# Graph block on one Trainium2 core: attention weights multiplied together before the items, slice tokens summed in turned form, a rewritten slice attention

## The reference, cut to what matters

```python
fx_mid = (x @ W_fx + b_fx).reshape(B, N, H, D).transpose(0, 2, 1, 3)
x_mid = (x @ W_x + b_x).reshape(B, N, H, D).transpose(0, 2, 1, 3)
slice_weights = jax.nn.softmax((x_mid @ W_slice + b_slice) / temp, axis=-1)
slice_norm = slice_weights.sum(axis=2)
slice_token = jnp.einsum('bhnc,bhng->bhgc', fx_mid, slice_weights)
slice_token = slice_token / (slice_norm[..., None] + 1e-05)
q = slice_token @ W_q
k = slice_token @ W_k
v = slice_token @ W_v
attn = jax.nn.softmax(jnp.einsum('bhgc,bhkc->bhgk', q, k) * SCALE, axis=-1)
out_slice = jnp.einsum('bhgk,bhkc->bhgc', attn, v)
out_x = jnp.einsum('bhgc,bhng->bhnc', out_slice, slice_weights)
return out_x.transpose(0, 2, 1, 3).reshape(B, N, INNER) @ W_out + b_out
```

## Time and profile before

| | us |
|---|---|
| median of 3 runs | 1682.46 (1680.82 to 1684.41) |
| the profiled execution's own time | 1682.33 |
| its span, first to last instruction | 1680.6 |
| PE busy | 1391.1 (83%) |
| VectorE (DVE) busy | 1310.9 (78%) |
| POOL busy | 1111.6 (66%) |
| ScalarE (ACT) busy | 665.2 (40%) |

### The profile page before, as it was taken

How to read it: one execution, slowest core, us unless ns; L and a number is a source line. 1 busy time by engine, 2 the same in 40 slices (tenths; PEclk the granted TensorE clock), 3 DMA queues, 4 the chain that set the end, 5 groups by cost and what they waited for, 6 DMA issues and landing times. The chain is left out here.

```text
span 1680.6 us, 27556 instructions
## 1 busy us (share of the span) xinstructions
PE 1391.1 (83%) x8473; PEld 1102.6 (66%) x8473; DVE 1310.9 (78%) x3978; ACT 665.2 (40%) x1867; POOL 1111.6 (66%) x1196
## 2 busy tenths in 40 slices
PE   5399989984788889888888888888989888886798
PEld 3277767763567777766666666666767666664587
DVE  8999879973588887888888888888787887873244
ACT  0144333420455454555455454455454544531000
POOL 1078888886777777777777777777777777720000
PEclk9699999985799998999999899899998999997599
DMA  9011112113444444444444444444444444512722
GB/s 231 9 58 53 43 41 65 48 37 87 118 124 123 123 125 124 123 123 127 119 123 123 118 122 123 123 122 124 124 121 124 121 121 116 150 51 68 267 74 72
DMA packets 106322, 180.11 MB, mean 107 GB/s; under 512 B 29183, under 2 KB 77694, under 8 KB 106175
## 3 DMA queue, kind: packets, MB, share of 16 engines
q0 software_dynamic: 44384, 113.26, 26.0%
...
...
## 5 line engine op out<-in xcount | busy, mean ns | idle before, releaser
L1043 POOL DMA_INDIRECT big<-node_table,rest x850 | 826.6, 972 | 245.4 <-issue 231.9
L1114 PE MATMUL psum<-big 128*125 128x257 f32 x1700 | 437.2, 415 | 73.7 <-DVE big L1615 73.7
L1114 PEld LDWEIGHTS psum<-big 128*125 128x125 f32 x1700 | 342.9, 207 | 139.6 <-DVE big L1615 80.5
L1262 ACT ACTIVATE rest<-big,rest 128x125 f32<-128x125 bf16 x850 | 268.3, 490 | 165.8 <-DVE rest L1563 164.7
L1615 DVE TENSOR_SCALAR big<-big,rest 128x125 f32<-128x125 bf16 x850 | 172.8, 293 | 0.0
L327 POOL DMA_INDIRECT edge_groups<-rest x112 | 143.9, 1285 | 27.2 <-issue 21.8
L1570 DVE TENSOR_REDUCE rest<-rest 128x125 f32<-128x2125 f32 x50 | 118.3, 2367 | 32.2 <-ACT rest L1262 32.2
L1253 ACT COPY big<-psum 125x1024 bf16<-125x1024 bf16 x150 | 103.8, 763 | 38.4 <-PE psum L1091 38.4
L1149 PE MATMUL psum<-big 125*128 125x256 f32 x416 | 101.1, 387 | 0.0
L1135 PE MATMUL psum<-rest,big 128*125 128x512 f32 x208 | 99.7, 601 | 0.0
L1759 PE MATMUL psum<-rest,big 128*125 128x256 f32 x400 | 88.7, 384 | 2.0 <-DVE rest L1812 2.0
...
## 6 DMA issues: line engine op xcount, KB each, us to landing
big<-node_table,rest POOLq DMA_INDIRECT x850
...
```

The lines of the kernel that those rows point to most:

```text
L1043: pool.indirect_dma_start(Gt[:, u, q * TW:(q + 1) * TW], None, table, bass.IndirectOffsetOnAxis(ap=item[:, u, 2 * q:2 * q + 1], axis=0)).t ...
L1114: mm = pe.matmul(bank[bAgg][0:R, 0:D + 1], P[:, u, q, :], Gt[:, u, q * TW:q * TW + D + 1], start=q == 0, stop=q == Q - 1)
L1262: act.activation(V[:, :, q], O[:, u, q, 0:R], ACT.Copy, scale=score[:, u, q:q + 1]).then_inc(s_v, 1)
```

## The change

Six things differ; line numbers in this section's rows are those of each kernel's own file.

- The seven attention weights are loaded by SP at the start of the items stage, behind the loads for the `W_x` fold and ahead of the items' own loads, and no longer after the last item.
- Ahead of the items TensorE turns `Wq`, `Wk`, `Wv`, makes `Wqk` (the product of query and key weights) and `Wvo` (value weights times output weights, per head), which ScalarE copies over `Wq` and `Wo`. The zeroing of the accumulators waits for that.
- `tokens` holds a 128-column piece of `y` as stationary operand and moves the 512 columns of `L`: two matmuls, and the sum is turned (256 x 512). The four zero matmul records that closed the sum (L1237) are gone.
- The attention needs no turning of the tokens. The norm is spread to rows by matmuls with the identity, `sT` is divided by it in one pass; `Wqk` replaces the queries and keys, `Wvo` the values and the output projection; the division by the softmax total goes to the copy of `M2`. VectorE's steps go from 21 to 14, with ScalarE taking half of some copies.
- All 50 loads of weight tiles are issued by SP, and the output stores by ScalarE.
- `total` and `res` share memory with the attention's tiles.

```diff
-        bfx, spare_row = rows2[0:1], rows2[32:33]
+        bfx, spare_row = rows2[0:FH, 0:G], rows2[32:33]
         Wq, Wk, Wv = a.take(G, G), a.take(G, G), a.take(G, G)
         Wo = a.take(G, FH, D)
+        Wqk, Wvo = Wq, Wo
...
+            turned_w = b.take(G, 3, G)
...
+                    attention_weights = ((Wfx, W_fx.rearrange("(c p) n -> p c n", p=128)), (bfx, b_fx.rearrange("(h c) -> h c", h=FH)), (Wq, W_q),
+                                         (Wk, W_k), (Wv, W_v), (Wo, W_out.rearrange("(h c) d -> c h d", h=FH)),
+                                         (bout, row(b_out).to_broadcast([R, D])))
+                    for to, of in attention_weights:
+                        sp.dma_start(to, of).then_inc(aw_in, 16)
...
+                    pe.wait_ge(aw_in, 112)
+                    for i, w in enumerate((Wq, Wk, Wv)):
+                        mm = pe.transpose(bank[7][0:G, i * G:(i + 1) * G], w, ident[0:G, 0:G])
+                    mm.then_inc(fw_psum, 1)
+                    pe.wait_ge(folded, 1)
+                    pe.matmul(bank[7][0:G, 256:256 + G], turned_w[:, 0, :], turned_w[:, 1, :], start=True, stop=True
+                              ).then_inc(fw_psum, 1)
+                    for i in range(IC):
+                        if i == IC - 1:
+                            pe.wait_ge(folded, 2)
+                        pe.matmul(bank[(0, 1, 2, 7)[i]][0:G, :], turned_w[:, 2, :],
+                                  Wo[:, 2 * i:2 * i + 2, :].rearrange("c h d -> c (h d)"), start=True, stop=True
+                                  ).then_inc(fw_psum, 1)
                     pe.wait_ge(fw_done, 19)
+                    pe.wait_ge(folded, 2 + IC)
...
-                    def tokens(n, u):
-
-                        for c in range(IC):
-                            mm = pe.matmul(bank[bSum + c // 2][:, (c % 2) * D:(c % 2 + 1) * D], L[:, c * 128:(c + 1) * 128],
-                                           y[:, u, :], start=False, stop=False, skip_group_check=True)
+                    def tokens(n, u, last=False):
+
+                        for c in range(DC):
+                            mm = pe.matmul(bank[bSum + c][:, :], y[:, u, c * 128:(c + 1) * 128], L, start=False, stop=last,
+                                           skip_group_check=True)
                         mm.then_inc(sum_psum, 1)
...
-                    tokens(last + 1, (TAIL + 1) % U)
-                    for b in range(2):
-                        mm = pe.matmul(bank[bSum + b][:, :], zero_row[:, 0:128], zero_row, start=False, stop=True,
-                                       skip_group_check=True)
-                    mm.then_inc(sum_psum, 1)
-                    pe.wait_ge(sum_psum, last + 3)
+                    tokens(last + 1, (TAIL + 1) % U, True)
+                    pe.wait_ge(sum_psum, last + 2)
...
+                    act.wait_ge(fw_psum, 3)
+                    act.copy(turned_w.rearrange("c i n -> c (i n)"), bank[7][0:G, 0:3 * G]).then_inc(folded, 1)
+                    act.wait_ge(fw_psum, 4)
+                    act.copy(Wqk, bank[7][0:G, 256:256 + G]).then_inc(folded, 1)
+                    for i in range(IC):
+                        act.wait_ge(fw_psum, 5 + i)
+                        act.copy(Wvo[:, 2 * i:2 * i + 2, :].rearrange("c h d -> c (h d)"), bank[(0, 1, 2, 7)[i]][0:G, :]
+                                 ).then_inc(folded, 1)
...
...
         with ExitStack() as _:
             a = Arena(rest, after_m2, REST_W)
...
+            tail_at = a.at
+            tokT = a.take(128, DC, INNER)
+            sT, sA, P, PT = (a.take(G, INNER) for _ in range(4))
+            Z = a.take(G, FH, D)
+            den_row, norm_rows = a.take(G, INNER), a.take(FH, INNER)
             den = a.take(128, IC)
...
+            ptop, ptot, pinv = a.take(G, FH), a.take(G, FH), a.take(128, IC)
+            ap, ad, ae = sem("attn_psum"), sem("attn_done"), sem("attn_copied")
             OB = 5
+            a = Arena(rest, tail_at, REST_W)
             total, res = a.take(R, OB, D), a.take(R, OB, D)
             o_psum, o_sum, o_done = (sem(n) for n in ("o_psum", "o_sum", "o_done"))
             o_out = [sem(f"o_out{u}") for u in range(OB)]
 
...
             with nc.Block() as block:
                 @block.sync
                 def _(sp):
...
                     for t in range(T):
...
+                        job = sp.value_load(job_of[0:1, t:t + 1], min_val=1, max_val=ITEMS + 1)
+                        sp.dma_start(SW[:, t].rearrange("p c r -> p (c r)"),
+                                     sw_store[bass.ds(job, 1)].rearrange("c p f -> (c p) f")).then_inc(sw_in[t // SW_GROUP], 16)
+
+                def head(h):
                     return slice(h * G, (h + 1) * G)
+
+                half = INNER // 2
 
                 @block.tensor
                 def _(pe):
...
                     for i in range(IC):
...
+                        mm = pe.matmul(bank[1][0:FH, i * 128:(i + 1) * 128], slice_norm[:, i:i + 1].to_broadcast([128, FH]),
+                                       ident, start=True, stop=True)
                     mm.then_inc(ap, 1)
...
+                    pe.wait_ge(ad, 2)
+                    for i in range(IC):
+                        mm = pe.matmul(bank[0][0:G, i * 128:(i + 1) * 128], den[:, i:i + 1].to_broadcast([128, G]), ident,
+                                       start=True, stop=True)
+                    mm.then_inc(ap, 1)
+                    pe.wait_ge(ad, 4)
+                    pe.matmul(bank[2][0:G, :], bfx, norm_rows, start=True, stop=False, skip_group_check=True)
+                    pe.wait_ge(ae, 1)
                     for h in range(FH):
                         for c in range(DC):
...
+                            mm = pe.matmul(bank[2][0:G, head(h)], Wfx[:, c, head(h)], tokT[:, c, head(h)], start=False,
+                                           stop=c == DC - 1, skip_group_check=True)
                     mm.then_inc(ap, 1)
...
+                    pe.wait_ge(ad, 5)
+                    pe.matmul(bank[3][0:G, 0:half], Wqk, sT[:, 0:half], start=True, stop=True)
+                    pe.matmul(bank[4][0:G, 0:half], Wqk, sT[:, half:], start=True, stop=True).then_inc(ap, 1)
+                    pe.wait_ge(ad, 6)
+                    pe.wait_ge(ae, 3)
                     for h in range(FH):
...
+                        mm = pe.matmul(bank[0][0:G, head(h)], sA[:, head(h)], sT[:, head(h)], start=True, stop=True)
                     mm.then_inc(ap, 1)
+
+                    def values(i):
+
+                        for h in (2 * i, 2 * i + 1):
+                            mm = pe.matmul(bank[4 + i][0:G, (h % 2) * D:(h % 2 + 1) * D], sT[:, head(h)], Wvo[:, h, :],
+                                           start=True, stop=True)
+                        mm.then_inc(ap, 1)
+
+                    values(0)
+                    values(1)
+                    pe.wait_ge(ae, 4)
+                    for h in range(FH):
+                        mm = pe.transpose(bank[1][0:G, head(h)], P[:, head(h)], ident[0:G, 0:G])
+                    mm.then_inc(ap, 1)
+                    values(2)
+                    values(3)
                     pe.wait_ge(ad, 10)
                     for h in range(FH):
...
+                        lo, i = (h % 2) * G, h // 2
+                        if h % 2 == 0:
+                            pe.wait_ge(ae, (5 + i if i < 2 else 8))
+                        mm = pe.matmul(bank[2 + i][lo:lo + G, 0:D], PT[:, head(h)], Z[:, h, :], start=True, stop=True)
+                        if h % 2:
+                            mm.then_inc(ap, 1)
+                    pe.wait_ge(ad, 14)
+                    pe.wait_ge(ae, 10)
                     for t in range(T):
                         if t % SW_GROUP == 0:
                             pe.wait_ge(sw_in[t // SW_GROUP], 16 * SW_GROUP)
@@ -1762,9 +1788,25 @@
 
                 @block.scalar
                 def _(act):
...
+                    act.copy(tokT[:, 1, :], bank[bSum + 1][:, :]).then_inc(ae, 1)
+                    act.wait_ge(ap, 2)
+                    act.copy(den_row, bank[0][0:G, :]).then_inc(ae, 1)
+                    act.wait_ge(ap, 4)
+                    act.copy(sA[:, half:], bank[4][0:G, 0:half]).then_inc(ae, 1)
+                    act.wait_ge(ad, 8)
+                    act.activation(P, P, ACT.Exp, scale=SLICE_SCALE).then_inc(ae, 1)
+                    for i in range(IC):
+                        act.wait_ge(ap, (6 + i if i < 2 else 7 + i))
+                        act.copy(Z[:, 2 * i:2 * i + 2, :].rearrange("k h d -> k (h d)"), bank[4 + i][0:G, :]).then_inc(ae, 1)
                     act.wait_ge(ad, 12)
...
+                    for i in range(2, IC):
+                        act.wait_ge(ap, 11 + i)
+                        act.activation(M2[:, i, :], bank[2 + i][:, 0:D], ACT.Copy, scale=pinv[:, i:i + 1]).then_inc(ae, 1)
+                    for t in range(T):
+                        act.wait_ge(o_done, t + 1)
```

(22 more changed lines are left out.)

83 lines of the change are left out of this document (1 added, 82 removed).

## The result

The changed kernel takes 1659.0 us in the median of 5 runs (1656.9 to 1663.1), the kernel before 1683.1 beside it: the ratio is 0.986, 95% interval 0.984 to 0.988. Two repeats of it gave 0.985 (0.983 to 0.987) and 0.986 (0.984 to 0.987). The forecast was 1666.1 with a range from 1660 to 1671. The sign and the place of the gain were right; it is 24 us and not 16.

The account below looks back on a forecast made before the run. POOL's gathers were taken to end the items, with the output's TensorE matmuls last in the chain. Gains of 1.2 + 1.2 + 13.0 + 0.8 = 16.2 off 1682.33 gave 1666.1 us, range 1660 to 1671.

Parts of the forecast that it names:

- What bounds the kernel: Whole kernel: POOL's gathers set when the items end; the output's 88.75 us of TensorE matmuls can only start earlier.
- The attention: Between items and output: with fewer VectorE steps, 40.5 us becomes 27.5 at the low clock, gain 13.0, 1.5 either way.
- The clock at its start: First matmuls of the attention: the last tokens can leave TensorE's clock high for the three spreads, gain 0.8, between 0 and 2.6.
- Rival 1: Attention: TensorE runs warm at 2.4 GHz; wholly, 1653.5 us, chance 0.06; for a part, 1659 to 1663, chance 0.12.
- Closing records: End of the items stage: without the four zero records VectorE sets the end, gain 1.2, between 1 and 1.6.
- Hold-up by the late loads: Last items: attention weight loads delayed gathers near 1445; loading them earlier gains 1.2, between 0 and 3.
- Products: Ahead of the items: weight products make the first item 2.3 us late, POOL's slack covers it, cost 0.
- the other engines alone need 20.4 us an item: Items: period of the engines besides POOL, against POOL's 21.8, so they regain 1.4 us with every item.
- rival 4: Items: turned tokens or a colder clock lift the engines' period past POOL's 21.8 us; from 22.2 no gain; chance 0.02.
- Loads and stores: Around attention and output: one queue feeds the output's loads fast enough, cost 0; ScalarE's store issues cost 0.1.

## Why the prediction was right and where it was wrong

- **What bounds the kernel** held: no matmul of the output got shorter (387 ns in the mean for 384), POOL never waited for a buffer, and the output has no wait for loads (0.6 us of idle time in all).
- **The attention, 13.0**: right in mechanism and nearly in size, 14.4. It was worked out for the low clock, and at the low clock the new sequence takes 26.15 us where I had 27.5; `W_fx` was the piece too dear, 5.0 for a measured 3.7: I had taken 0.62 a head from a sequence in which L1727 follows each head's L1726.
- **The clock at its start, 0.8**: the step that failed. I bounded it by 0 and 2.6, the three spreads alone. It measured 26.15 less 20.2, **5.9 us**: the clock stayed at 1.00 for 9 us, through the spreads, `W_fx`, `Wqk` and the scores. The row that I held against it, 5.00 of 5.00 busy at 0.50, shows only that a low clock can stay low. That it would be high at 1546 the rows could have told: the closing records ran four times 512 columns in 1.98 us, the high pace, right up to the pause of 3 us that the change removes. That it would stay high for 9 us they could not: with the closing records put back it was as high at the start and fell 0.5 us later. What decides between the two is open. Rival 1 for a part, 1659 to 1663, was the case that came, and had 0.12. That the median lies at its edge is partly chance, since the items stage, below, brought some 2 us that no term had.
- **Closing records, 1.2**: supported (1.4 us in the trace of the turned tokens alone, where taking them out left a total of 0.5 to 5 us less); what they may do to the clock had no term.
- **Hold-up by the late loads, 1.2**: not there. Moving the loads alone changed nothing. That the item at 1445 is long doesn't say that the end is.
- **Products, 0**: the reason was wrong, and the size probably, an estimated 0.9 to 2.2 lost, which no total shows. The failing step is "the other engines alone need 20.4 us an item": the row is right, and the kernel before keeps that pace up to its eighth item, but it is a run of items at the high clock, and the cycle that follows has a mean of 21.6. In the changed kernel the cycle begins at the third item, with a mean of 21.5 next to POOL's 21.8 before and 21.7 now. The 1.4 us an item that I had them regain are 0.2 to 0.3, and the engines never caught up. It is rival 4's colder clock in small: from 440 to 1480 it was 0.92 to 0.93, before 0.95 to 0.96.
- **Loads and stores, 0**: right as a term, and blind as a reason. I asked whether one queue was fast enough for the output and not what ScalarE had behind its 25 issues. Had the change left them there, it would have been slower than before.

Together, on the profiled execution: 14.4 for the steps and 5.9 for the clock make the attention's 20.3; the items stage gives 1.8, of which 1.3 lie between the last addition to the slice norm and the attention (0.83 us for 2.11), where the closing records stood; the later start of the stage (2.1) and the output and end (0.7) take back 2.9. That is the 19.2 of this execution. The medians of all runs differ by 24. This execution was late by 2.1 already at the start of its items, and its items stage, 1136.7, is the slowest of five; their mean is 1135.0, 2.1 less than the stage before, although the products are in it. With that mean the parts come to about 23. This gain had no term in the prediction. It goes with the shorter gathers below, and its cause is open.
